# Five unused buffers that shift the operands of the expert stage's matmuls in a fused graph-attention and mixture-of-experts kernel

## The chip, the cores and the metric

One core of a Trainium2 chip runs the whole program. The metric is the device time of one execution in microseconds (us); less is better. The kernel before took 2409.39 us (median of 3 runs, 2408.38 to 2410.31).

## The reference

```python
def _L0_gnn_ref(h, adj, W, a):
    Wh = jnp.einsum('bnd,df->bnf', h, W)
    s1 = Wh @ a[:DOUT, 0]
    s2 = Wh @ a[DOUT:, 0]
    e = s1[:, :, None] + s2[:, None, :]
    e = jnp.where(e > 0, e, ALPHA * e)
    e = e + jnp.log(adj + EPS)
    alpha_w = jax.nn.softmax(e, axis=-1)
    return jnp.einsum('bij,bjf->bif', alpha_w, Wh)

def _L0_ffn_ref(x, Wr, br, W1, b1, g1, be1, m1, v1, W2, b2, g2, be2, m2, v2, Wo, bo):
    feat = jnp.mean(x, axis=0)
    w = jax.nn.softmax(feat @ Wr + br, axis=-1)
    h = jnp.einsum('bfd,edh->bfeh', x, W1) + b1
    h = jax.nn.relu(_bn(h, g1, be1, m1, v1))
    h = jnp.einsum('bfeh,ehk->bfek', h, W2) + b2
    h = jax.nn.relu(_bn(h, g2, be2, m2, v2))
    y = jnp.einsum('bfeh,ehd->bfed', h, Wo) + bo
    return jnp.einsum('bfed,fe->bfd', y, w)

x = x + _L0_gnn_ref(_layernorm(x), adj, W, a)
x = x + _L0_ffn_ref(_layernorm(x), ...)
```

x and adj are 128 graphs of 128 nodes, x with 256 features. There are 8 experts, and each has three layers of 256 by 256.

## The kernel before, in words

The kernel has two stages. The first stage is the graph attention. It goes over 32 groups of 4 graphs, with plain fp32 matmuls (the projection at L721, the product with the attention weights at L738, transposes at L692, L763 and L772), and it also splits the weights of layers 1 and 2 into a high and a low part of type float32r. The second stage is the expert stage. It goes over 32 tiles of 512 nodes and over 8 experts in each tile, so 256 units of work.

In the expert stage a product of two fp32 matrices is made of three float32r matmuls: high times high, high times low, low times high. They add up in PSUM. Per unit TensorE does:

- layer 1 in Strassen's form (`strassen`, L1189): 7 block products, each 3 matmuls of 256 columns, so 21. The stationary operand (loaded as weights) is a 128x128 block of `wq_hi` or `wq_lo`, the moving one is a 256-column block of `xq_hi` or `xq_lo`;
- layer 2 (`product`, L168): 12 matmuls of 512 columns. Stationary: a block of `w_hi` or `w_lo`; moving: `h1_hi` or `h1_lo`;
- layer 3 (`layer_3`, L1213): 24 matmuls of 256 columns. Stationary: a 128-column block of the activations `h2_hi` or `h2_lo`; moving: a 256-column block of `wo_hi` or `wo_lo`.

Once a tile, eight fp32 transposes (L129) prepare the next tile. Every matmul has a weight load of its own ahead of it (PEld in the profile), also where the same block follows twice. The three layers of different experts are interleaved by hand on TensorE: block 0 of layer 1 of the new expert, first half of layer 3 of the expert three before, blocks 1 to 4 of layer 1, second half of layer 3, block 5, layer 2 of the expert one before, block 6. Between them ScalarE and VectorE finish sums (`v`, L994; `z`, L1075 and L1085), apply batch norm and ReLU (`h`, L1002), split activations into high and low parts (L989 and L1092 for `h1`, L1008 and L1098 for `h2`) and add each expert's output (L1115). TensorE waits for each of these by a semaphore. `keep_clock` (L1199) issues matmuls whose result isn't used, at the start of the expert stage.

The matmuls of the three layers, as the code has them:

```python
mm = nc.tensor.matmul(out_ps, w[:, e, q, :], x[:, q, :], ...)            # L1189, layer 1
mm = nc.tensor.matmul(acc_ps, w[:, i, c, cols], s[:, c, :], ...)         # L168, layer 2
mm = nc.tensor.matmul(ps_y[:, b4, :], h[:, c, cols], w[:, e, c, :], ...) # L1213, layer 3
```

SBUF buffers are laid out one behind another in the order in which they are declared, each start rounded up to a multiple of 32 bytes within a partition. All blocks of one operand start at multiples of 512 bytes from the buffer's start, because a 128-column fp32 block is 512 bytes in a partition. So within a layer the distance between the start of the stationary block and the start of the moving block, modulo 512, is the same in every matmul.

Of the kernel before, what the change touches and what calls it, by code (L numbers as in the profile page):

```python
# [24 lines left out]
P = 128  # L25
# [13 lines left out]
def adj_ffn(nc, x, adj, gnn_w, gnn_a, wr, br, w1, b1, g1, be1, m1, v1, w2, b2, g2, be2, m2, v2, wo, bo, out):  # L39
# [17 lines left out]
    with ExitStack() as ctx:  # L57
        def sb(name, shape, dt=F32, stack=ctx):
            return stack.enter_context(nc.sbuf_tensor(name, shape, dt))
# [5 lines left out]
        ident = sb("ident", [P, P])  # L65
        minus_half = sb("minus_half", [P, 2 * EC])
        half_cols = sb("half_cols", [P, GB])
        wq_hi = sb("wq_hi", [P, E, Q, P], F32R)
        wq_lo = sb("wq_lo", [P, E, Q, P], F32R)
        w_hi = sb("w_hi", [P, E, C, D], F32R)  # L70
# [17 lines left out]
        acc = resb  # L88
        x1t = sb("x1t", [P, GB, D])
        xs = sb("xs", [P, Q + 1, H])  # L90
        xq_hi = sb("xq_hi", [P, Q, H], F32R)
        xq_lo = sb("xq_lo", [P, Q, H], F32R)

# [691 lines left out]
        with ExitStack() as sbk:  # L785
            def sbb(name, shape, dt=F32):
                return sb(name, shape, dt, sbk)
# [22 lines left out]
            bias_out = sbb("bias_out", [P, D])  # L810
            v = sbb("v", [P, 3, H])
            z = sbb("z", [P, C, T])
            h1_hi = sbb("h1_hi", [P, C, T], F32R)
            h1_lo = sbb("h1_lo", [P, C, T], F32R)
            ysum = x1[1]
            h2_hi = [sbb(f"h2_hi{i}", [P, C, T], F32R) for i in range(2)]
            h2_lo = [sbb(f"h2_lo{i}", [P, C, T], F32R) for i in range(2)]
            wo_hi = sbb("wo_hi", [P, E, C, D], F32R)
            wo_lo = sbb("wo_lo", [P, E, C, D], F32R)

# [488 lines left out]
```

## Time and profile before

| | before |
|---|---|
| median of 3 runs | 2409.39 us (2408.38 to 2410.31) |
| the profiled execution's own time | 2407.3 us |
| its span (first to last instruction) | 2405.5 us |
| mean granted TensorE clock | 0.997 of full speed |
| TensorE matmul busy | 2376.4 us, 99% |
| VectorE busy | 1688.0 us, 70% |
| ScalarE busy | 1611.6 us, 67% |
| GpSimd busy | 428.9 us, 18% |
| matmuls | 16217 |

The profile gives for each engine the time in which it worked, groups of instructions by line, and a chain of work that ended last. A matmul's record is longer than the time it takes up in a row of matmuls, since the next one starts before it ends: what counts for time is from one start to the next, or a piece of the chain divided by the number of matmuls in it.

### The profile page before, as it was taken

What the parts mean: (1) busy time and instruction counts of PE and PEld (TensorE: products, weight loads), DVE (VectorE), ACT (ScalarE), POOL (GpSimd) and SP (SyncE); (2) the same over time, 40 slices, a digit from 0 to 9 for tenths busy, and PEclk for the clock granted to TensorE, in tenths of its full rate; (3) what the DMA queues carried; (4) which work ended last, traced back from release to release, by engine and by line L of the source; (5) the groups of instructions that cost most, each with busy time, mean ns of one, the idle gap of its engine ahead of it and who ended that gap; (6) DMA issues with size and microseconds to landing.
All of it is one profiled execution on the core that took longest, in us unless ns stands there. A gap on an engine that the chain in (4) does not pass through costs nothing.

```text
span 2405.5 us, 46160 instructions
## 1 busy us (share of the span) xinstructions
PE 2376.4 (99%) x16217; PEld 2192.5 (91%) x16217; DVE 1688.0 (70%) x2582; ACT 1611.6 (67%) x2522; POOL 428.9 (18%) x562
## 2 busy tenths in 40 slices
PE   8999899999999999999999999999999999999999
PEld 7778799999999999999999999999999999999998
DVE  6999766666666676666666666666666666666666
ACT  6888566666666666666666666666666666666665
POOL 5888411111110000111111100101111111001010
PEclk9999899999999999999999999999999999999999
DMA  6778300000000000000000000000000000000000
GB/s 219 235 256 291 103 27 27 26 26 26 26 26 26 26 17 17 18 26 26 26 26 26 26 26 26 17 17 17 26 26 26 26 26 26 26 26 17 17 10 27
DMA packets 91330, 116.42 MB, mean 48 GB/s; under 512 B 4728, under 2 KB 78880, under 8 KB 91296
## 3 DMA queue, kind: packets, MB, share of 16 engines
q1 hardware_dynamic: 91296, 115.99, 14.9%
q8 instruction: 19, 0.31, 0.1%
q14 instruction: 15, 0.12, 0.0%
HBM read 82.42 MB, written 33.55 MB: 48 GB/s over the span
## 4 chain that ended last, share of the span: by engine, by line
PE 90%; DVE 5%; issue 2%; ACT 1%; POOL 1%; DVEq 0%; DMA 0%; SPq 0%; ACTq 0%; POOLq 0%
PE ps_y L1213 30%; PE ps_wide L168 30%; PE ps_wide L1189 26%; PE ps_wide L721 1%; PE ps_t L129 1%; DVE resb L613 1%; DVE st L573 1%; PE ps_th L738 1%; DVE h L647 1%; DVE st L565 1%; DVE w_bc L647 1%; DVE l_sb L626 1%; DVE p_sb L659 0%; POOL dev L417 0%; ACT xnT L553 0%
## 5 line engine op out<-in xcount | busy, mean ns | idle before, releaser
L994 ACT ACTIVATE v<-ps_wide,bn_cols 128x256 f32<-128x256 f32 x768 | 433.6, 565 | 398.7 <-PE ps_wide L1189 259.5
L1002 ACT ACTIVATE h<-ps_wide,bn_cols 128x512 f32<-128x512 f32 x512 | 399.0, 779 | 325.6 <-PE ps_wide L168 323.4
L1213 PE MATMUL ps_y<-wo_lo,h_hi 128*128 128x256 f32 x2048 | 578.1, 282 | 0.0
L1213 PE MATMUL ps_y<-wo_hi,h_hi 128*128 128x256 f32 x2048 | 576.7, 282 | 0.5 <-DVE h_lo L1098 0.5
L1213 PE MATMUL ps_y<-wo_hi,h_lo 128*128 128x256 f32 x2048 | 576.7, 282 | 0.0
L1092 DVE SCALAR_TENSOR_TENSOR h_lo<-z,h_hi 128x1024 fp32r<-128x1024 f32 x256 | 314.0, 1226 | 343.6 <-ACT h_hi L989 343.6
L1189 PE MATMUL ps_wide<-xq_hi,wq_hi 128*128 128x256 f32 x1792 | 509.8, 284 | 6.5 <-DVE z L1075 3.4
L1189 PE MATMUL ps_wide<-xq_hi,wq_lo 128*128 128x256 f32 x1792 | 506.0, 282 | 0.0
L1189 PE MATMUL ps_wide<-xq_lo,wq_hi 128*128 128x256 f32 x1792 | 505.8, 282 | 0.0
L168 PE MATMUL ps_wide<-h_hi,w_hi 128*128 128x512 f32 x1024 | 404.7, 395 | 0.6 <-DVE h_lo L1092 0.6
L168 PE MATMUL ps_wide<-h_hi,w_lo 128*128 128x512 f32 x1024 | 405.1, 396 | 0.0
L168 PE MATMUL ps_wide<-h_lo,w_hi 128*128 128x512 f32 x1024 | 403.7, 394 | 0.0
L1213 PEld LDWEIGHTS ps_y<-wo_hi,h_lo 128*128 128x128 f32 x2048 | 390.0, 190 | 0.0
L1213 PEld LDWEIGHTS ps_y<-wo_lo,h_hi 128*128 128x128 f32 x2048 | 389.0, 190 | 0.0
L1213 PEld LDWEIGHTS ps_y<-wo_hi,h_hi 128*128 128x128 f32 x2048 | 387.8, 189 | 1.1 <-DVE h_lo L1098 0.7
L1098 DVE TENSOR_TENSOR h_lo<-h,h_hi 128x1024 fp32r<-128x1024 f32 x256 | 313.4, 1224 | 99.0 <-ACT h_hi L1008 99.0
L973 POOL TENSOR_TENSOR resb<-resb,w_bc 128x512 f32<-128x512 f32 x64 | 86.7, 1356 | 1571.3 <-DMA resb<-x_scratch 1564.2
L1189 PEld LDWEIGHTS ps_wide<-xq_hi,wq_hi 128*128 128x128 f32 x1792 | 339.6, 190 | 18.6 <-DVE z L1075 3.9
L1189 PEld LDWEIGHTS ps_wide<-xq_hi,wq_lo 128*128 128x128 f32 x1792 | 338.6, 189 | 10.5
L1189 PEld LDWEIGHTS ps_wide<-xq_lo,wq_hi 128*128 128x128 f32 x1792 | 339.4, 189 | 0.0
L1115 DVE SCALAR_TENSOR_TENSOR resb<-ps_y,w_node,resb 128x512 f32<-128x512 f32 x448 | 332.9, 743 | 3.9 <-PE ps_y L1213 3.9
L1085 DVE SCALAR_TENSOR_TENSOR z<-ps_wide,bn_cols,v 128x512 f32<-128x512 f32 x256 | 191.9, 750 | 173.5 <-PE ps_wide L1189 173.4
(138 smaller groups left out, 2997.4 us busy)
## 6 DMA issues: line engine op xcount, KB each, us to landing
x_sb<-in_x SPq DMA_DIRECT2D x32, 512.0 KB, 4.1
res<-in_x SPq DMA_DIRECT2D x32, 512.0 KB, 6.0
x1t<-x_scratch SPq DMA_DIRECT2D x32, 512.0 KB, 3.3
resb<-x_scratch SPq DMA_DIRECT2D x32, 512.0 KB, 3.3
out<-resb SPq DMA_DIRECT2D x31, 512.0 KB, 3.0
adj_sb<-in_adj SPq DMA_DIRECT2D x32, 256.0 KB, 6.2
x_scratch<-h SPq DMA_DIRECT2D x16, 512.0 KB, 5.0
x_scratch<-w_bc SPq DMA_DIRECT2D x16, 512.0 KB, 4.8
```

Source lines behind the costliest of these rows:

```text
L129: last = nc.tensor.transpose(ps_x[:, c, b4 * N:(b4 + 1) * N], x1t[:, b4, c * P:(c + 1) * P], ident[:, :])
L168: mm = nc.tensor.matmul(acc_ps, w[:, i, c, cols], s[:, c, :], start=start and n == 0, stop=stop and n == len(terms) - 1)
L647: last = nc.vector.scalar_tensor_tensor(out=x1[q][:, b4, :], in0=ps_h[:, b4, :], scalar=rinv[:, b4:b4 + 1], in1=res[q][:, b4, :], op0=ALU. ...
L973: nc.gpsimd.tensor_tensor(resb[:, g, :], resb[:, g, :], ysum[:, g, :], ALU.add).then_inc(resb_done, 1)
L994: nc.scalar.activation(v[:, slot, :], ps_l1[:, 0, 0:H], ACT.Identity, bias=bn_cols[:, 1, cols], scale=bn_cols[:, 0, cols]).then_inc(done, 1)
L1002: nc.scalar.activation(h2[:, m, :], ps_l2[:, m, :], ACT.Relu, bias=bn_cols[:, 3, cols], scale=bn_cols[:, 2, cols]).then_inc(r2_done, 1)
L1085: nc.vector.scalar_tensor_tensor(out=z[:, 0, :], in0=ps_l1[:, 1, :], scalar=bn_cols[:, 0, C * e:C * e + 1], in1=v[:, 0:2, :].rearrange("p ...
L1092: nc.vector.scalar_tensor_tensor(out=h1_lo[:, :, :], in0=z[:, :, :], scalar=0.0, in1=h1_hi[:, :, :].bitcast(F32), op0=ALU.max, op1=ALU.sub ...
L1098: nc.vector.tensor_tensor(h2_lo[u[1] % 2][:, :, :], h2[:, :, :], h2_hi[u[1] % 2][:, :, :].bitcast(F32), ALU.subtract).then_inc(lo2_done, 1)
L1115: nc.vector.scalar_tensor_tensor(out=dst[:, g, :], in0=ps_y[:, g, :], scalar=w_node[:, e:e + 1], in1=old, op0=ALU.mult, op1=ALU.add).then_ ...
L1189: mm = nc.tensor.matmul(out_ps, w[:, e, q, :], x[:, q, :], start=start and n == 0, stop=stop and n == len(terms) - 1, skip_group_check=True)
L1213: mm = nc.tensor.matmul(ps_y[:, b4, :], h[:, c, cols], w[:, e, c, :], start=(k == 0 and b4 % per_bank == 0), stop=(k == len(terms) - 1 and ...
```

## The change

Five buffers are declared that nothing reads or writes. Each is put just ahead of an operand buffer and moves it and all that is declared behind it. No instruction is added, removed or put in another order; only addresses differ.

```diff
@@ -65,6 +65,7 @@
         half_cols = sb("half_cols", [P, GB])
+        sb("shift_wq", [P, 24])
         wq_hi = sb("wq_hi", [P, E, Q, P], F32R)
@@ -88,6 +89,7 @@
         xs = sb("xs", [P, Q + 1, H])
+        sb("shift_xq", [P, 80])
         xq_hi = sb("xq_hi", [P, Q, H], F32R)
@@ -810,11 +812,14 @@
             z = sbb("z", [P, C, T])
+            sbb("shift_h1", [P, 24])
             h1_hi = sbb("h1_hi", [P, C, T], F32R)
             h1_lo = sbb("h1_lo", [P, C, T], F32R)
             ysum = x1[1]
+            sbb("shift_h2", [P, 16])
             h2_hi = [sbb(f"h2_hi{i}", [P, C, T], F32R) for i in range(2)]
             h2_lo = [sbb(f"h2_lo{i}", [P, C, T], F32R) for i in range(2)]
+            sbb("shift_wo", [P, 112])
             wo_hi = sbb("wo_hi", [P, E, C, D], F32R)
```

Worked out from the declarations, the start of each operand within its partition, in bytes modulo 512 (the high and the low part are alike):

| layer | stationary, before | moving, before | stationary minus moving, before | stationary, now | moving, now | stationary minus moving, now |
|---|---|---|---|---|---|---|
| 1 | wq 288 | xq 416 | -128 | wq 384 | xq 320 | +64 |
| 2 | w 288 | h1 320 | -32 | w 384 | h1 320 | +64 |
| 3 | h2 320 | wo 320 | 0 | h2 384 | wo 320 | +64 |

Other buffers move too, by 96 bytes (`w_stage`, `x1t`, `resb`, `w_bc` and their neighbours) or by 416 (the first stage's `x_sb`, `res`, `adj_sb`, `wh`, `pT` and the rest of its own buffers). All starts stay multiples of 32 bytes.

## Rows read from the trace of the kernel before

**Rows 1.** The page's first part, and its slices for matmul and granted clock.

```profile
PE 2376.4 (99%) x16217; PEld 2192.5 (91%) x16217; DVE 1688.0 (70%) x2582; ACT 1611.6 (67%) x2522; POOL 428.9 (18%) x562
...
PEclk9999899999999999999999999999999999999999
```

**Rows 2.** Busy time by stretches: the first stage, and the expert stage.

```profile
core 0: us, PE busy (x) PEld busy (x) DVE busy (x) ACT busy (x) POOL busy (x), PEclk, DMA share, GB/s
...
0.00:262.00 262.00, 244.58 (x1313) 205.87 (x1314) 239.49 (x787) 206.79 (x558) 201.19 (x355) 0.99 0.76 241
300.00:2400.00 2100.00, 2099.14 (x14730) 1958.01 (x14729) 1420.46 (x1739) 1387.08 (x1935) 214.36 (x192) 1.00 0.07 24
```

**Rows 3.** The page's chain that ended last, by engine and by line.

```profile
PE 90%; DVE 5%; issue 2%; ACT 1%; POOL 1%; DVEq 0%; DMA 0%; SPq 0%; ACTq 0%; POOLq 0%
PE ps_y L1213 30%; PE ps_wide L168 30%; PE ps_wide L1189 26%; PE ps_wide L721 1%; PE ps_t L129 1%; DVE resb L613 1%; DVE st L573 1%; PE ps_th L738 1%; DVE h L647 1%; DVE st L565 1%; DVE w_bc L647 1%; DVE l_sb L626 1%; DVE p_sb L659 0%; POOL dev L417 0%; ACT xnT L553 0%
```

**Rows 4.** The page's groups of instructions: one of three alike for each layer.

```profile
L1213 PE MATMUL ps_y<-wo_lo,h_hi 128*128 128x256 f32 x2048 | 578.1, 282 | 0.0
...
L1189 PE MATMUL ps_wide<-xq_hi,wq_lo 128*128 128x256 f32 x1792 | 506.0, 282 | 0.0
...
L168 PE MATMUL ps_wide<-h_hi,w_lo 128*128 128x512 f32 x1024 | 405.1, 396 | 0.0
```

**Rows 5.** The chain in order of time (start, duration), pieces of one unit.

```profile
1002.61 1.44 PE ps_y L1213 x12
1004.05 1.42 PE ps_wide L1189 x12
1005.47 1.42 PE ps_y L1213 x12
1006.89 0.36 PE ps_wide L1189 x3
1007.25 2.80 PE ps_wide L168 x12
1010.05 0.71 PE ps_wide L1189 x6
```

**Rows 6.** The same chain where the transposes of the next tile stand.

```profile
1034.51 0.87 PE ps_t L129 x8
```

**Rows 7.** Instructions in order of time (start, duration), TensorE at half clock.

```profile
272.68 1.48 PE L1199 MATMUL ps_y<-xq_hi,wq_hi 128*128 128x256 f32 x6
273.96 0.41 PE L1189 MATMUL ps_wide<-xq_hi,wq_hi 128*128 128x256 f32 x1
```

**Rows 8.** Busy time of that stretch, with its granted clock.

```profile
272.50:275.50 3.00, 3.00 (x17) 3.00 (x17) 0.46 (x3) 1.13 (x2) 2.11 (x8) 0.56 0.60 190
```

**Rows 9.** Instructions in order of time, TensorE: first stage's projection, 16 fp32 matmuls.

```profile
102.53 3.65 PE L721 MATMUL ps_wide<-gw,xnT 128*128 128x258 f32 x16
106.02 0.75 PE L763 MATMUL ps_pT<-ident,p_sb 128*128 128x128 f32 x4
```

**Rows 10.** Instructions in order of time: last matmul of a layer 2, then transposes.

```profile
1034.12 0.39 PE L168 MATMUL ps_wide<-h_hi,w_lo 128*128 128x512 f32 x1
1034.34 1.04 PE L129 MATMUL ps_t<-ident,x1t 128*128 128x128 f32 x8
```

**Rows 11.** Weight loads of single lines: durations in ns, shortest/median/longest.

```profile
L1213 PEld LDWEIGHTS ps_y<-wo_hi,h_lo x1840: 187/192/193, 399.9 to 2300.0; 128*128 128x128 f32 x184
...
L168 PEld LDWEIGHTS ps_wide<-h_hi,w_hi x920: 187/188/188, 404.0 to 2298.2; 128*128 128x128 f32 x184
...
L129 PEld LDWEIGHTS ps_t<-ident,x1t x248: 137/141/146, 307.1 to 2290.8; 128*128 128x128 f32 x124
```

**Rows 12.** Instructions in order of time: TensorE and VectorE within one unit.

```profile
1005.31 0.27 PE L1213 MATMUL ps_y<-wo_hi,h_hi 128*128 128x256 f32 x1
1005.40 1.22 DVE L1092 SCALAR_TENSOR_TENSOR h_lo<-z,h_hi 128x1024 fp32r<-128x1024 f32 x1 [0.26 <-ACT h_hi L989]
1005.42 0.28 PE L1213 MATMUL ps_y<-wo_lo,h_hi 128*128 128x256 f32 x1
...
1007.09 0.39 PE L168 MATMUL ps_wide<-h_hi,w_hi 128*128 128x512 f32 x1
...
1008.34 0.74 DVE L1075 SCALAR_TENSOR_TENSOR z<-ps_wide,bn_cols,v 128x512 f32<-128x512 f32 x1
...
1009.89 0.28 PE L1189 MATMUL ps_wide<-xq_hi,wq_hi 128*128 128x256 f32 x1
```

## The prediction

> **What bounds the kernel now.** I read the page's first part, then the stretches, the chain, and last the chain's pieces in order of time. TensorE has a matmul in flight 99% of the span, at full granted clock nearly everywhere [rows 1]. The first stage, up to 262 us, leaves TensorE idle in places and has VectorE busy for 239 of 262 us; the expert stage has TensorE busy for 2099 of 2100 us, with VectorE at 1420 and ScalarE at 1387 [rows 2]. The chain is TensorE for 90%, and the three layers alone are 30 + 30 + 26% of it [rows 3]. So in the expert stage time is the number of matmuls times the spacing from one start to the next, and nothing else.
>
> The numbers: layer 3 has 3 x 2048 = 6144 matmuls, layer 1 has 3 x 1792 = 5376, both of 256 columns, and layer 2 has 3 x 1024 = 3072 of 512 [rows 4]. The spacing, from the pieces of one unit: layer 3 1.44 and 1.42 us for 12, so 118 to 120 ns; layer 1 1.42 for 12, 118 ns; layer 2 2.80 for 12, 233 ns [rows 5].
>
> What should these be? 256 columns at 2.4 GHz are 107 ns, 512 are 213. Three other rows run close to such a figure. Eight fp32 transposes, each with its weight load, take 0.87 us, 109 ns each [rows 6]; a plain fp32 matmul spends twice the time per column, so 128 columns there are 107 ns too. Sixteen fp32 matmuls of 258 columns take 106.02 - 102.53 = 3.49 us, 218 ns each, against 215 of columns [rows 9]. And layer 1's own kind of matmul, at the half clock (granted 0.56 in that stretch, so near the 1.2 GHz level), takes (273.96 - 272.68) / 6 = 213 ns, exactly its columns, with the operands 128 bytes apart as they always are [rows 7, 8]. **Only float32r at full clock loses time**: 9 to 11 ns in each matmul of 256 columns, and 233 - 216 = 17 ns in each of 512. Over the program that is 5376 x 9.4 + 6144 x 10.5 + 3072 x 17 = 51 + 65 + 52 = 168 us.
>
> What could lose it? During a matmul TensorE streams the moving operand, 4 bytes a column in each partition, and also loads the next stationary block: loads are in flight for 1958 of the 2100 us [rows 2]. At full clock float32r asks for 1024 bytes per 107 ns, twice what it asks in the rows without loss. The load fetches 512 bytes in at most the same time. If SBUF is divided into banks that repeat every 512 bytes, the moving stream, being twice as fast, runs through the load's bank about once per load, and where in the load this happens depends on the distance that the change sets. That is my mechanism; no row shows the banks themselves.
>
> **The change part by part.**
>
> *The five unused buffers.* No instruction is added or moved, on any queue, and no wait. Their direct cost is nothing.
>
> *Layers 1 and 3: the distance goes from -128 and from 0 to +64.* The trace has no matmul at +64 at full float32r rate, so I bound it. Below: 109 ns [rows 6]. Above: 0.12 us from start to start is common, and a load of layer 3 lasts up to 193 ns against 187 at its shortest [rows 11], so a load stretched in every matmul would give some 119 + 4 = 123 ns. Between them, the same code does reach 1005.42 - 1005.31 = 0.11 us [rows 12], so collisions aren't the same in each matmul and a better place exists. I take 115 ns, four below the mean of 119, between that good case and today's. That is 11520 x 4 = 46 us.
>
> *Layer 2: from -32 to +64.* Below: 216 ns, above 237 by the same stretch of 4 ns. One row stands nearest: the last matmul of layer 2 ahead of the transposes takes 1034.34 - 1034.12 = 0.22 us instead of 0.233 [rows 10], and what differs is that the load under it is a transpose's short one, 141 ns of record against 188 [rows 11]. So part of layer 2's loss hangs on the load, and about 4 ns of it is what a shorter overlap gives back; most of it doesn't go even then. I take 229 ns, 3072 x 4 = 12 us.
>
> *What is late next.* A faster TensorE shortens the cover of ScalarE's and VectorE's chains. Two are tight: `h1_lo` ends at 1005.40 + 1.22 = 1006.62 and layer 2 starts at 1007.09, 0.47 us later; `z` ends at 1009.08 and block 6 starts at 1009.89, 0.8 us later [rows 12]. The six pieces of a unit add up to 8.15 us [rows 5], and 4 ns in each of its 57 matmuls takes 0.23 us from the unit; less than half lies over either chain. So nothing is late. If the whole loss went (0.65 us per unit) the first would keep about 0.1 us. Cost nothing; if the cover were gone, 0.1 us in 256 units is 26 us.
>
> *First stage and other buffers.* Its fp32 matmuls run at 218 ns where 215 are columns [rows 9], and TensorE doesn't bound it. Buffers for DMAs move by 96 or 416 bytes; VectorE covers the DMAs there. I put it at 0, and 1 us to either side.
>
> **Sum.** 2407.3 (the profiled execution, 1.8 over its span) - 46 - 12 = 2349. That execution is 2 us below the median of the runs, so about 2351 beside the median; I say 2350.
>
> **The rivals.**
>
> *No effect.* The loss may belong to the stream and not to the load: a feed that can't quite keep 9.6 bytes per ns. For it: today's three distances, -128, -32 and 0, lose 9.4, 17 and 10.5 ns, and 17 on twice the columns is less than 2 x 10.5, so no distance stands out and the loss grows with columns [rows 5]. The long part of layer 2's loss that remains under a short load [rows 10] speaks the same way. Against: it has to explain why two matmuls of the same kind differ, 0.11 and 0.12 us. Time: 2407 to 2409. The Trainium skill, in "TensorE: Matmul & The Clock Gate", section "Step-by-step: what each phase is for", says that the moving operand and the weight load have independent SBUF read ports and that loading the next weights takes nothing from the running matmul. By that rule the change does nothing and the sum is 2407; the half-clock and fp32 rows agree with it, the full-clock float32r rows are its test.
>
> *The whole loss goes.* If +64 takes the two streams past each other altogether, each matmul falls to 109 or 216 ns: 2407 - 168 = 2239. For it: the rows without loss do reach these figures with loads under way. Against: a stream twice as fast as the load, over the length of a load, must meet it once in a period of 512 bytes wherever they start.
>
> *Slower: the moving stream starts right behind the load.* With the stationary block 64 bytes ahead in the bank order, the moving stream, which starts at about the same moment, may catch it in the first 64 bytes, in every matmul, and trail it. Price: 4 ns more in each, the spread of the load records [rows 11], 14592 x 4 = 58, so 2465, and half of that, 2436, if the collision costs only one of the two streams. The point from which it decides: whether the stream has already drawn 64 bytes (7 ns) when the load begins to read. For it: that distance lies nearest to a start in step. Against: layer 3 already has both starts equal, distance 0, and loses no more than layer 1 at -128.
>
> *The change doesn't do what it says.* The sizes (96, 320, 96, 64, 448 bytes) are multiples of 32, and the starts worked out from them give +64 in each layer. I give this nothing of its own.
>
> **How the numbers follow.** The forecast, some of the loss gone (2290 to 2395): 0.44. The whole or nearly the whole gone: 0.12. No effect: 0.22. Slower: 0.22. So faster by over 0.2% 0.56, within 0.2% (about 5 us, what a measurement of this kernel can tell from no change) 0.22, slower 0.22. Range: 2285 to 2440 takes in the forecast, no effect and the milder half of slower, and leaves out about 0.1 at either end. Signs on both sides hold much of the chance; the forecast's own range is 2290 to 2395.
>
> **What would show it.** Right: the piece of 12 layer 3 matmuls at 1.38 us, layer 1 the same, layer 2's at 2.75; TensorE still at 99% or so, with all the gain between 300 us and the end; load records at their shortest, 187 ns, everywhere. Wrong by no effect: the pieces read 1.42 and 2.80 again. Wrong by the slower rival: pieces of 1.47 and more, and loads of 193 ns or longer in all three layers. Wrong in the size: pieces near 1.31 and 2.60, and then waits on `h1_lo` ahead of layer 2. The first stage's end, near 262 us, should not move by more than 1 us.

## The result and the profile after

The changed kernel takes 2349.91 us (median of 4) against 2409.61 before: ratio 0.9755, 95% interval 0.9742 to 0.9768. One of its four executions took 2390.89 us and is left out of the ratio, as are one execution of the run with every start 32 bytes further (2394.13 us) and one of the last run (3873.8 us, at a granted clock of 0.556); none of the three has a trace. The profiled execution took 2350.85 us with a span of 2349.1, against 2407.3 and 2405.5.

Every line number after the first added buffer is one or more higher: layer 3 is now L1218, layer 1 L1194, layer 2 L170, the transposes L131.

The page's first part, and busy time by stretches (the lines that answer to [rows 1, 2]):

```profile
PE 2318.5 (99%) x16217; PEld 2134.5 (91%) x16217; DVE 1687.9 (72%) x2582; ACT 1608.8 (68%) x2522; POOL 426.8 (18%) x562
...
PEclk9999999999999999999999999999999999999999
```

```profile
0.00:262.00 262.00, 245.14 (x1309) 206.62 (x1310) 237.03 (x781) 205.48 (x553) 199.47 (x347) 0.99 0.76 241
262.00:300.00 38.00, 28.61 (x153) 23.82 (x152) 27.85 (x58) 17.43 (x32) 14.61 (x24) 0.91 0.26 83
300.00:2340.00 2040.00, 2039.63 (x14718) 1899.28 (x14717) 1418.93 (x1739) 1384.58 (x1937) 212.68 (x192) 1.00 0.07 24
```

TensorE still fills the expert stage (2039.63 of 2040 us), with the same work on VectorE and ScalarE (1419 and 1385 us against 1420 and 1387). No other engine has become the bound, and the gain is in the spacing of matmuls. But the records of neighbouring matmuls overlap, so a matmul that starts a little late leaves no gap in this busy time. The chain's pieces of one unit, against [rows 5]:

```profile
1000.04 1.36 PE ps_y L1218 x12
1001.40 1.36 PE ps_wide L1194 x12
1002.76 1.36 PE ps_y L1218 x12
1004.12 0.34 PE ps_wide L1194 x3
1004.46 2.79 PE ps_wide L170 x12
1007.25 0.69 PE ps_wide L1194 x6
```

Twelve matmuls of 256 columns take 1.36 us, 113.3 ns each, in layer 1 and in layer 3 alike; before it was 1.42 to 1.44. Layer 2 reads 2.79 against 2.80: it gained nothing. The unit is 7.90 us instead of 8.15, and 256 units of 0.25 us are 64 us, against 56.4 us of span.

The rest stands in three places. First, one unit of each tile, the fifth, starts its layer 2 late:

```profile
987.03 1.22 DVE L1097 SCALAR_TENSOR_TENSOR h_lo<-z,h_hi 128x1024 fp32r<-128x1024 f32 x1 [0.26 <-ACT h_hi L994]
...
988.38 0.19 PEld L170 LDWEIGHTS ps_wide<-h_hi,w_hi 128*128 128x128 f32 x1
988.39 0.49 PE L170 MATMUL ps_wide<-h_hi,w_hi 128*128 128x512 f32 x1
988.72 0.39 PE L170 MATMUL ps_wide<-h_lo,w_hi 128*128 128x512 f32 x1
```

`h1_lo` ends at 987.03 + 1.22 = 988.25 us, the first weight load of layer 2 starts at 988.38, and its second matmul starts 0.33 us after its first, where 0.23 is usual. This happens in all 31 tiles that follow transposes, each time with the first matmul 0.12 to 0.14 us behind the end of `h1_lo`, and costs 3.2 us in all. Before, only the very last layer 2 of the program started so.

Second, the transposes of the first tile (whose weight loads start at 307.1 us before) come later, because the first stage ended later in this execution:

```profile
L131 PEld LDWEIGHTS ps_t<-ident,x1t x248: 138/141/142, 308.4 to 2236.2; 128*128 128x128 f32 x124
```

That need not be an effect of the buffers. Two later runs (layer 2 at -64 and at 0 by moving h1) have every buffer of the first stage where it is here, and these loads start at 307.2 us in the one and at 308.9 us in the other.

Third, some units are slower again, although every address is what it was. The chain near the end:

```profile
2271.61 1.36 PE ps_y L1218 x12
...
2273.31 2.83 PE ps_wide L170 x12
...
2276.85 1.41 PE ps_y L1218 x12
```

From 2276.85 us on the same twelve matmuls of layer 3 take 1.41 us. That second figure, 1.41, turned out to be the key to the case. Counting shorter stretches of it near 374, 1634 and 1659 us, some 13 of the 256 units have it.

Summed over the start times in the two traces, from the first tile's transposes on, layer 1 takes 605.6 us where it took 633.0, layer 3 696.3 where it took 729.3, and layer 2 710.4 where it took 707.7. That is 57.7 us less, and with the start 1.4 us later it gives the 56.4 us (rounded) by which the spans differ.

### The profile page after: what moved, and what is told of

It is laid out like the page before. It is cut to its first block, busy times and chain, and to the rows that moved or that the text cites. A ratio compares the mean times of both kernels' runs of the same rounds, so it can differ in the third digit from the quotient of the medians.

```text
span 2349.1 us, 46160 instructions
## 1 busy us (share of the span) xinstructions
PE 2318.5 (99%) x16217; PEld 2134.5 (91%) x16217; DVE 1687.9 (72%) x2582; ACT 1608.8 (68%) x2522; POOL 426.8 (18%) x562
## 4 chain that ended last, share of the span: by engine, by line
PE 89%; DVE 5%; issue 2%; POOL 1%; DMA 1%; ACT 1%; DVEq 0%; SPq 0%; POOLq 0%; ACTq 0%
PE ps_wide L170 30%; PE ps_y L1218 30%; PE ps_wide L1194 26%; PE ps_wide L723 1%; PE ps_t L131 1%; DVE resb L615 1%; DVE st L575 1%; DVE st L567 1%; DVE h L649 1%; DVE w_bc L649 1%; PE ps_th L740 1%; DVE l_sb L628 1%; DVE p_sb L661 0%; DMA adj_sb<-in_adj 0%; POOL dev L419 0%
## 5 line engine op out<-in xcount | busy, mean ns | idle before, releaser
L1218 PE MATMUL ps_y<-wo_hi,h_hi 128*128 128x256 f32 x2048 | 566.0, 276 | 0.6 <-DVE h_lo L1103 0.6
L1218 PE MATMUL ps_y<-wo_lo,h_hi 128*128 128x256 f32 x2048 | 565.8, 276 | 0.0
L1218 PE MATMUL ps_y<-wo_hi,h_lo 128*128 128x256 f32 x2048 | 565.8, 276 | 0.0
L1097 DVE SCALAR_TENSOR_TENSOR h_lo<-z,h_hi 128x1024 fp32r<-128x1024 f32 x256 | 314.0, 1226 | 344.1 <-ACT h_hi L994 344.1
L1194 PE MATMUL ps_wide<-xq_hi,wq_hi 128*128 128x256 f32 x1792 | 501.0, 280 | 7.3 <-DVE z L1080 3.5
L1194 PE MATMUL ps_wide<-xq_hi,wq_lo 128*128 128x256 f32 x1792 | 496.0, 277 | 0.0
L1194 PE MATMUL ps_wide<-xq_lo,wq_hi 128*128 128x256 f32 x1792 | 495.9, 277 | 0.0
L170 PE MATMUL ps_wide<-h_hi,w_hi 128*128 128x512 f32 x1024 | 407.1, 398 | 0.8 <-DVE h_lo L1097 0.8
L170 PE MATMUL ps_wide<-h_hi,w_lo 128*128 128x512 f32 x1024 | 405.0, 396 | 0.0
L170 PE MATMUL ps_wide<-h_lo,w_hi 128*128 128x512 f32 x1024 | 404.9, 395 | 0.0
L1218 PEld LDWEIGHTS ps_y<-wo_hi,h_hi 128*128 128x128 f32 x2048 | 384.5, 188 | 1.2 <-DVE h_lo L1103 0.8
L1218 PEld LDWEIGHTS ps_y<-wo_lo,h_hi 128*128 128x128 f32 x2048 | 384.8, 188 | 0.0
L1218 PEld LDWEIGHTS ps_y<-wo_hi,h_lo 128*128 128x128 f32 x2048 | 384.5, 188 | 0.0
L1103 DVE TENSOR_TENSOR h_lo<-h,h_hi 128x1024 fp32r<-128x1024 f32 x256 | 313.3, 1224 | 66.9 <-ACT h_hi L1013 66.1
L1194 PEld LDWEIGHTS ps_wide<-xq_hi,wq_hi 128*128 128x128 f32 x1792 | 337.3, 188 | 19.2 <-DVE z L1080 4.2
L1194 PEld LDWEIGHTS ps_wide<-xq_hi,wq_lo 128*128 128x128 f32 x1792 | 337.7, 188 | 10.6
L1194 PEld LDWEIGHTS ps_wide<-xq_lo,wq_hi 128*128 128x128 f32 x1792 | 337.3, 188 | 0.0
```

The costliest lines, as they stand in the source:

```text
L1097: nc.vector.scalar_tensor_tensor(out=h1_lo[:, :, :], in0=z[:, :, :], scalar=0.0, in1=h1_hi[:, :, :].bitcast(F32), op0=ALU.max, op1=ALU.sub ...
L1103: nc.vector.tensor_tensor(h2_lo[u[1] % 2][:, :, :], h2[:, :, :], h2_hi[u[1] % 2][:, :, :].bitcast(F32), ALU.subtract).then_inc(lo2_done, 1)
L1194: mm = nc.tensor.matmul(out_ps, w[:, e, q, :], x[:, q, :], start=start and n == 0, stop=stop and n == len(terms) - 1, skip_group_check=True)
```

## The experiments

My theory at this point: each layer's spacing follows from its own distance, stationary start minus moving start modulo 512, and 256-column matmuls have a good place at +64. The first rivals: alignment of the starts, and a rhythm of the whole sequence that one layer sets for the others. All runs are the kernel before with buffers that nothing uses, unless said otherwise; the diffs show those buffers by name and size, and the buffer that follows each.

### Layer 3 alone

```diff
+            sbb("shift_h2", [P, 16])
             h2_hi = [sbb(f"h2_hi{i}", [P, C, T], F32R) for i in range(2)]
+            sbb("shift_wo", [P, 112])
             wo_hi = sbb("wo_hi", [P, E, C, D], F32R)
```

> Only layer 3 gets the distance +64 (h2 at 384, wo at 320 modulo 512); layer 1 stays at -128 and layer 2 at -32. Distance theory: the pieces of 12 layer 3 matmuls go from 1.42-1.44 to 1.36 us, layer 1 stays at 1.42 and layer 2 at 2.80; 6144 matmuls x 6.2 ns = 38 us, so about 2371 us. Rival, that one layer's addresses set the phase in which the whole sequence locks: layer 1 changes too. Rival, that the gain came from 64-byte alignment of the layer 1 weights (288 is no multiple of 64): nothing changes, 2409 us.

Measured: 2372.36 us, ratio 0.9853 (0.9836 to 0.9869). The pieces:

```profile
1000.17 1.37 PE ps_y L1215 x12
1001.54 1.41 PE ps_wide L1191 x12
...
1004.68 2.79 PE ps_wide L168 x12
```

Layer 3 gets most of what it has in the changed kernel, and the time is the one worked out for it alone. Layer 1 moved by about 0.01 us, which at this point looked like noise. It wasn't: summed over the trace, of 36.7 us less layer 3 has 26.6, layer 1 8.2 and layer 2 1.9, so the time came out for a partly different reason, and the rival that one layer's addresses change another layer's spacing had its first evidence here.

### All distances at +64, every start 32 bytes further

```diff
+        sb("shift_wq", [P, 32])
         wq_hi = sb("wq_hi", [P, E, Q, P], F32R)
+        sb("shift_xq", [P, 80])
         xq_hi = sb("xq_hi", [P, Q, H], F32R)
+            sbb("shift_h1", [P, 24])
             h1_hi = sbb("h1_hi", [P, C, T], F32R)
+            sbb("shift_h2", [P, 16])
             h2_hi = [sbb(f"h2_hi{i}", [P, C, T], F32R) for i in range(2)]
+            sbb("shift_wo", [P, 112])
             wo_hi = sbb("wo_hi", [P, E, C, D], F32R)
```

> All three distances are +64 as in the changed kernel, but every operand starts 32 bytes later, so that none is at a multiple of 64. Distance theory: as the changed kernel, pieces of 1.36, 1.36 and 2.79 us, 2350 us. Alignment theory: pieces back to 1.42 and more, 2405 us or above.

Measured: 2347.38, 2348.54 and 2351.37 us in three of four executions, ratio 0.9759 (0.9739 to 0.9779), pieces as in the changed kernel:

```profile
1001.14 1.36 PE ps_wide L1194 x12
1002.50 1.36 PE ps_y L1218 x12
...
1004.21 2.79 PE ps_wide L170 x12
```

No start is a multiple of 64 bytes here, and moving all operands on by 32 bytes together changes nothing. Alignment to 64 bytes is out: what counts is where operands lie to one another.

### All at -64, and a mixture

The sizes were chosen for the starts 352 (wq, w, h2) and 416 (xq, h1, wo).

```diff
+        sb("shift_wq", [P, 16])
         wq_hi = sb("wq_hi", [P, E, Q, P], F32R)
+        sb("shift_xq", [P, 112])
         xq_hi = sb("xq_hi", [P, Q, H], F32R)
+            sbb("shift_h1", [P, 24])
             h1_hi = sbb("h1_hi", [P, C, T], F32R)
+            sbb("shift_h2", [P, 112])
             h2_hi = [sbb(f"h2_hi{i}", [P, C, T], F32R) for i in range(2)]
+            sbb("shift_wo", [P, 16])
             wo_hi = sbb("wo_hi", [P, E, C, D], F32R)
```

> All three distances are -64, the mirror of the changed kernel. Theory that the sign matters (the stationary block has to lie ahead in the bank order): pieces of 1.42 us and more, 2405 us or above. Theory that only the distance from 0 matters: 1.36 us and 2350 us. For layer 2, which did not change between -32 and +64, I expect 2.80 again.

Measured: 2382.54 us (one execution), neither of the two times expected. Layers 1 and 3 at 1.41, layer 2 at 2.75:

```profile
1003.63 1.41 PE ps_y L1218 x12
1005.04 1.41 PE ps_wide L1194 x12
...
1008.22 2.75 PE ps_wide L170 x12
```

The mixture has wq and w at 384, xq at 352, h1 at 256, h2 at 416, wo at 320:

```diff
+        sb("shift_wq", [P, 24])
         wq_hi = sb("wq_hi", [P, E, Q, P], F32R)
+        sb("shift_xq", [P, 88])
         xq_hi = sb("xq_hi", [P, Q, H], F32R)
+            sbb("shift_h2", [P, 40])
             h2_hi = [sbb(f"h2_hi{i}", [P, C, T], F32R) for i in range(2)]
+            sbb("shift_wo", [P, 104])
             wo_hi = sbb("wo_hi", [P, E, C, D], F32R)
```

> Layer 1 at +32, layer 2 at +128, layer 3 at +96. If a collision costs the same wherever it falls, layer 1 and layer 3 read as at +64, 1.36 us for 12. If +64 is a narrow good place, one of the two or both go back to 1.42 us. Layer 2: 2.80 us if its loss belongs to the moving stream, less if it depends on the distance and +128 is a good place. Each piece is read by itself; the time is then 2350 to 2410 us.

Measured: 2398.59 us (one execution): layer 1 at +32 reads 1.41 to 1.42, layer 3 at +96 1.41 to 1.44, layer 2 at +128 2.80. So +64 looked like a narrow good place for 256 columns, and -64 like a better one for layer 2, 4 ns a matmul. I had expected layer 2 to stay at 2.80 there: a miss.

### Each layer at its best distance

```diff
+        sb("shift_wq", [P, 24])
         wq_hi = sb("wq_hi", [P, E, Q, P], F32R)
         wq_lo = sb("wq_lo", [P, E, Q, P], F32R)
+        sb("shift_w", [P, 96])
         w_hi = sb("w_hi", [P, E, C, D], F32R)
+        sb("shift_xq", [P, 112])
         xq_hi = sb("xq_hi", [P, Q, H], F32R)
```

(h1, h2 and wo get the buffers of the changed kernel.)

> Layers 1 and 3 at +64 as in the changed kernel, layer 2 at -64, where the run with all distances at -64 had its shortest spacing (229 ns against 233 to 234 at -32 and +64). Distance theory, each layer by itself: pieces of 1.36 us for layers 1 and 3, 2.75 for layer 2, so 3072 x 4.7 = 14 us less than the changed kernel: 2335 us. Rival, that layer 2's spacing hangs on the phase in which layer 1 hands over: 2.79 again, 2350 us.

Measured: 2384.73 us, ratio 0.9893 (0.9876 to 0.9909): 35 us slower than the changed kernel, where 14 us less was expected.

```profile
1001.92 2.76 PE ps_wide L171 x12
...
1005.38 1.41 PE ps_y L1219 x12
1006.80 1.41 PE ps_wide L1195 x12
```

Layer 2 has what was hoped for. But layers 1 and 3, at the same +64 as in the changed kernel, are back at 1.41. **Here the theory that each layer follows its own distance fell.**

### The old distances, exchanged, and three new ones

```diff
+        sb("shift_xq", [P, 96])
         xq_hi = sb("xq_hi", [P, Q, H], F32R)
+            sbb("shift_h1", [P, 24])
             h1_hi = sbb("h1_hi", [P, C, T], F32R)
+            sbb("shift_h2", [P, 104])
             h2_hi = [sbb(f"h2_hi{i}", [P, C, T], F32R) for i in range(2)]
+            sbb("shift_wo", [P, 32])
             wo_hi = sbb("wo_hi", [P, E, C, D], F32R)
```

> The distances of before change places: layer 1 at 0, layer 2 at 0, layer 3 at -128. Distance theory: layer 1 then reads what layer 3 had at 0 (120 ns where it runs long), layer 3 what layer 1 had at -128 (118 to 120). Theory that the layers differ by what they do: each keeps its own figure. Time about 2405 us in both; layer 2 at 0 is new, between 229 and 236 ns.

Measured: 2384.15 us (one execution), where 2405 was expected. Layers 1 and 3 read 1.42 and 1.43, as before, and layer 2 at 0 reads 2.73, the shortest so far. Most of the gain is layer 2's: (2.80 - 2.73) / 12 is 5.8 ns, times 3072 is 18 of the 25 us.

```profile
1003.01 1.43 PE ps_y L1217 x12
1004.44 1.42 PE ps_wide L1193 x12
...
1007.63 2.73 PE ps_wide L169 x12
```

The next has xq at 480, h1 at 96, h2 at 64, and the rest as before:

```diff
+        sb("shift_xq", [P, 16])
         xq_hi = sb("xq_hi", [P, Q, H], F32R)
+            sbb("shift_h1", [P, 56])
             h1_hi = sbb("h1_hi", [P, C, T], F32R)
+            sbb("shift_h2", [P, 120])
             h2_hi = [sbb(f"h2_hi{i}", [P, C, T], F32R) for i in range(2)]
+            sbb("shift_wo", [P, 64])
             wo_hi = sbb("wo_hi", [P, E, C, D], F32R)
```

> Layer 1 at -192, layer 2 at +192, layer 3 at -256 (the same as +256). If the banks repeat every 256 bytes, layer 1 at -192 is the same as +64 and reads 1.36 us for 12, and layer 3 at -256 the same as 0, 1.43 us. If they repeat every 512 and +64 is a single good place, both read 1.40 to 1.44. Layer 2 at +192 equals -64 under a period of 256 and would read 2.75 us; otherwise 2.78 to 2.83.

Measured: 2377.08 us (one execution). Layer 1 at -192 1.37, layer 3 at -256 1.42 to 1.43, layer 2 at +192 2.76. All three are what a period of 256 bytes would give. But after the run before this one a single figure no longer stands for a distance, so I don't take the period as shown; it stays open. Layer 1 reads 1.37 here between pieces of layer 3 at 1.42 and more, as layer 3 alone at +64 read 1.37 between pieces of layer 1 at 1.41: a layer can take up its short spacing anew within the unit.

### A short load under each third matmul

Addresses as before. Layers 1 and 3 are changed in the same way. The output rows 32 to 127 miss the second of each three terms.

```diff
-                mm = nc.tensor.matmul(acc_ps, w[:, i, c, cols], s[:, c, :], ...)
+                wide = P if n % 3 != 1 else 32
+                mm = nc.tensor.matmul(acc_ps[0:wide], w[:, i, c, m * P:m * P + wide], s[:, c, :], ...)
```

> Addresses as in the kernel before. The second of each three matmuls in all three layers loads and computes only 32 of its 128 stationary columns, so that 96 of 128 output rows miss the product of the terms that it carries; all matmuls stream as many columns as before. Under the first of each three the load is then a short one. Theory that the loss is a collision of the moving stream with the load: the spacing after the first of three falls to about 109 ns (256 columns) and 216 ns (512), the others stay near 119 and 233. Rival, a feed too slow for float32r at full clock whatever is loaded: 119 and 233 ns everywhere.

Measured: 2386.27 us (one execution), pieces of 1.41, 1.41 and 2.78. Matmuls of layer 2 in order of time:

```profile
1000.34 0.39 PE L169 MATMUL ps_wide<-h_hi,w_hi 128*128 128x512 f32 x1
1000.57 0.40 PE L169 MATMUL ps_wide<-h_lo,w_hi 128*32 128x512 f32 x1
1000.80 0.40 PE L169 MATMUL ps_wide<-h_hi,w_lo 128*128 128x512 f32 x1
1001.04 0.40 PE L169 MATMUL ps_wide<-h_hi,w_hi 128*128 128x512 f32 x1
```

The short load (a record of 108 ns against 188) runs under the first matmul, which takes 0.23 us to the next start, like its neighbours. The average over the trace from 400 to 2200 us is finer: 229.8 ns, against 233.3 and 232.8 for the other two. So in layer 2 a load of 32 columns instead of 128 gives back some 3 ns of the 17, where a collision with the load should have given back all. In layers 1 and 3 the first of three takes 117.2 and 118.3 ns, where that theory wanted 109. Neither theory's numbers hold. Shortening loads did take 23 us off the whole, so loads aren't without effect either; whether by their length or by the rhythm that the next section finds, this run doesn't show.

### Only layer 2's weights back to +64

```diff
+        sb("shift_wq", [P, 24])
         wq_hi = sb("wq_hi", [P, E, Q, P], F32R)
+        sb("shift_stage", [P, 96])
         w_stage = sb("w_stage", [P, Q + 1, P])
+        sb("shift_xq", [P, 112])
         xq_hi = sb("xq_hi", [P, Q, H], F32R)
```

(as the run with each layer at its best, with the 384 bytes behind `w_lo` instead of ahead of `w_hi`)

> As the run best_per_layer, which kept layers 1 and 3 at +64 and yet lost their gain (2384.7 us), except that layer 2's weights go back to +64; every other operand, the transposes' input too, lies at exactly the addresses of that run. If layer 2's distance is what spoils the other layers: pieces of 1.36 us again and 2350 us. If it was something else (the distance modulo 1024, the place of the transposes' input): 2385 us and pieces of 1.41 again.

Measured: 2370.35 us (one execution), halfway between the two times that were expected, and the chain says why. Pieces of one execution, end of one tile, transposes, start of the next:

```profile
1015.56 1.41 PE ps_wide L1195 x12
1016.98 1.41 PE ps_y L1219 x12
1018.39 0.35 PE ps_wide L1195 x3
1018.74 2.79 PE ps_wide L171 x12
1021.54 0.87 PE ps_t L132 x8
1022.41 0.70 PE ps_wide L1195 x6
1023.11 1.36 PE ps_y L1219 x12
1024.47 1.36 PE ps_wide L1195 x12
...
1081.25 1.36 PE ps_y L1219 x12
1082.95 2.79 PE ps_wide L171 x12
1085.74 0.87 PE ps_t L132 x8
1087.32 1.41 PE ps_y L1219 x12
1088.73 1.41 PE ps_wide L1195 x12
```

From 1023.11 to 1081.25 us all 24 pieces of twelve 256-column matmuls read 1.36, across seven layers 2. At the very same addresses the next tile runs at 1.41, and so on in turn, with the change at the transposes each time from 437 us on. So at +64 matmuls of 256 columns have **two rhythms**, 113.3 and 117.5 ns, and mostly keep the one they are in. Layer 2 at +64 mostly hands on either rhythm unchanged; the transposes, with another kind of load and stream, often change it.

It isn't a law, as the changed kernel's own trace shows: 29 of its 31 transposes are followed by the short rhythm. Twice it falls into the long one in the middle of a tile, and both times right behind a layer 2 that started late for `h1_lo` (its pieces read 2.90 us at 1630.55 and 2.83 at 2273.31), but most of the late ones leave the short rhythm as it is. And twice it goes back to the short one across an ordinary layer 2 (at 379 and 1664 us).

### Layer 2 at -64 and at 0 by moving h1

The changed kernel's other buffers stay; the one ahead of `h2_hi` gets the size that keeps h2 at 384.

```diff
+            sbb("shift_h1", [P, 56])
             h1_hi = sbb("h1_hi", [P, C, T], F32R)
+            sbb("shift_h2", [P, 112])
             h2_hi = [sbb(f"h2_hi{i}", [P, C, T], F32R) for i in range(2)]
```

> The changed kernel with layer 2 at -64 reached by moving its moving operand h1 (448) instead of its weights. Layers 1 and 3 keep +64 and layer 1's buffers keep their addresses. Theory that TensorE locks into one of two rhythms at +64 and that layer 2 hands over the wrong one: 1.41 us pieces and 2385 us as in best_per_layer. Theory that each layer follows its own distance: 1.36 and 2.75 us, 2336 us.

Measured: 2378.56 us (one execution), near the 2385 of the two-rhythm theory. In its trace the first unit of each of the 31 tiles is in the short rhythm and the other seven in the long one, and 31 units of 45 matmuls x 4.2 ns are the 6 us between the two figures. In the second variant the buffer ahead of `h1_hi` is `[P, 40]`, and there is none ahead of `h2_hi`:

> The changed kernel with layer 2 at 0, where another run gave its shortest spacing (226 to 227 ns), by moving h1 to 384. If layers 1 and 3 stay in the rhythm of 113.3 ns: 3072 x 6.5 = 20 us less than the changed kernel, 2330 us. If the hand-over from layer 2 puts them in the other rhythm of 117.8 ns: 11520 x 4.5 = 52 us more, less those 20, about 2382 us.

Measured: 2373.57 us, ratio 0.9849 (0.9833 to 0.9866). The unit after the transposes, and the next:

```profile
1025.59 1.36 PE ps_y L1217 x12
1026.94 1.36 PE ps_wide L1193 x12
...
1030.01 2.73 PE ps_wide L170 x12
...
1033.45 1.41 PE ps_y L1217 x12
1034.86 1.41 PE ps_wide L1193 x12
1036.27 1.41 PE ps_y L1217 x12
```

The transposes put this tile, and every second one, in the short rhythm, and the first layer 2 at distance 0 ends it: layer 2 itself runs at 226.7 ns (2.72 to 2.73 us), and hands over the long one. The transposes' input lies where the changed kernel has it, so its place isn't what makes tiles alternate.

### Layer 2 at 0 by its weights

```diff
+        sb("shift_w", [P, 112])
         w_hi = sb("w_hi", [P, E, C, D], F32R)
+        sb("shift_stage", [P, 16])
         w_stage = sb("w_stage", [P, Q + 1, P])
```

(beside the buffers of the changed kernel)

> Layer 2 at 0 again, but by moving its weights (320) and not h1; the transposes' input lies as in the changed kernel modulo 512. In the step from layer 2 back to layer 1 the stream of h1 (320) now meets a load of wq (384), +64, where it was 0 in the run l2_zero. If the rhythm of 113.3 ns is lost because of that step's distance, it now holds over all tiles and the time is 2330 us. If it is lost because of the distance inside layer 2, each tile has it for one unit at most and the time is about 2373 us again.

Measured: 2374.72, 2382.46 and 2383.52 us in three of four executions, ratio 0.9890 (0.9868 to 0.9911). The trace is of the first, with pieces of 1.41 and 2.75; the first unit of each of its 31 tiles is in the short rhythm and the rest in the long one. So the distance in the step back to layer 1 isn't what ends the short rhythm. In all four runs where layer 2 had another distance than +64 beside two layers at +64, it ran faster inside and the short rhythm was gone after one layer 2 at the latest; whether its speed or its distance does that isn't separated. And layer 2 at 0 reads 2.75 here and 2.73 in the run before, so its own distance alone doesn't fix its spacing either. No version tried beats the changed kernel. That one gives up some 20 us in layer 2 and keeps the 48 of the short rhythm (11520 x 4.2 ns).

## Why the prediction was right

**What bounds it** held: TensorE has a matmul in flight nearly throughout, and all the gain lies between 300 us and the end.

**The time was right to 1 us, and that was luck.** The terms of the sum erred against each other: 46 + 12 = 58 us were forecast and 56.4 came, but as 60.4 in layers 1 and 3, 2.6 lost again in layer 2, and 1.4 of later start.

- *Layers 1 and 3, 4 ns each, 46 us.* Over the trace 27.4 and 33.0 us, so 5.1 and 5.4 ns each. The bound from below (109 ns) isn't reached: 113.3 stays.
- *Layer 2, 4 ns each, 12 us.* Wrong. Its pieces read 2.79 against 2.80, where the sign asked for was 2.75, and over the trace it takes 2.6 us more: 0.6 less by its spacing, 3.2 more by the late starts. The term came from a last matmul of layer 2 that takes 0.22 us (229 ns by its unrounded start times) above a transpose's short load [rows 10], read as "4 ns is what a shorter overlap gives back". The change makes no load shorter; and in the changed kernel the same matmul above the same short load takes 1014.99 - 1014.75 = 0.24 us.

```profile
1014.75 0.40 PE L170 MATMUL ps_wide<-h_hi,w_lo 128*128 128x512 f32 x1
1014.99 1.04 PE L131 MATMUL ps_t<-ident,x1t 128*128 128x128 f32 x8
```

- *First stage, 0 with 1 us to either side.* It ended 1.4 us later, within what executions with the same addresses there differ by (307.2 and 308.9 us).
- *Nothing late next, cost nothing.* Wrong, by 3.2 us. The step that failed is "less than half lies over either chain". The time from the end of `h1_lo` to the first matmul of layer 2 is 1.18 us in most units before and 0.94 us now: the whole 0.25 us of a unit came off it. In the tightest unit, the one that the prediction had read at 0.47 us [rows 12], it fell to 0.13 us with layer 2 starting 0.1 us late. The price was there, as "if the cover were gone, 0.1 us in 256 units"; it fell due in one unit of eight. The busy share of 2039.63 in 2040 us hides it.

**The mechanism** was right in its first half: the relative place of operands changes the spacing, with no instruction changed, and a move of all by 32 bytes doesn't. Its second half, one collision per load at a place that the distance fixes, was wrong: the same addresses give 113.3 or 117.5 ns according to what ran before. The 0.11 us from which the prediction took that "a better place exists" is no sign of either: in that trace a spacing of 112 or 113 ns in layer 3 stands only behind the first matmul of a half that follows layer 1, once in every unit, so it belongs to the hand-over. Banks and collisions themselves were not seen; that a short load under a matmul of layer 2 gives back 3 ns of 17 speaks against their simplest form. Nor is it separated whether the other engines' accesses take part, since the buffers also move for them; VectorE's records are as long as before (`h1_lo` 1226 ns and `h2_lo` 1224 on average, in both).

**The rivals.** No effect fell. The Trainium skill says in "TensorE: Matmul & The Clock Gate", section "Step-by-step: what each phase is for", that loading the next weights takes nothing from the running matmul. By that rule, as the prediction read it, addresses alone don't move the time, and here they moved it by 2.4%. Whether it is the load that takes from the matmul, or which part of the path is shared, the runs don't show. The whole loss gone: no, 4 ns above 109 stay in 256 columns and 17 above 216 in 512. Slower by a collision at the start: not at +64; the load records of layer 3, 187 to 193 ns before [rows 11], now read 188 in the median:

```profile
L1218 PEld LDWEIGHTS ps_y<-wo_hi,h_lo x2048: 187/188/192, 300.6 to 2345.4; 128*128 128x128 f32 x187
```

## What to carry to other kernels

Where TensorE is without a gap and float32r matmuls at full clock take more than their columns (here 118 to 120 ns for 256, 107 being columns), the spacing can be tuned by unused buffers alone: 0.25 us of an 8.15 us unit here. Read twelve matmuls of each kind from the chain's pieces and not the busy time, and test a new layout in the whole sequence: a layer's best distance by itself (layer 2 at 0 or at -64) cost 24 to 35 us in all, because it put its neighbours in a worse rhythm. Read a wait from start to start too, in the tightest unit of a tile: matmul records overlap, and the busy share showed nothing of 3.2 us. And look at several executions: a rhythm that is kept and not forced may be the other one next time.

## What the runs showed of the hardware that was not expected

- *Two rhythms at the same addresses.* 256-column float32r matmuls with their loads run at 113.3 or at 117.5 ns in the same execution (1.36 and 1.41 us for 12), keep it over dozens of matmuls and mostly through a layer 2 at +64, and change mostly at the transposes. The changed kernel's own last units are in the long one. The 2390.89 us of one of its executions, and the 2394.13 us of one with every start 32 bytes further, would fit a stay there from start to end (2350 + 11520 x 4.2 ns less what is in it already and less the late starts is some 2393 us, an estimate); without a trace of either that is only argued. They are two of the eight executions that have all three layers at +64.
- *Steps.* The steady spacings are 113.3 and 120 ns (1.44 us for 12, before) for 256 columns and 226.7 ns (2.72) for 512: the columns' time plus one, two and two times 6.7 ns, that is 16 cycles of 2.4 GHz. The long rhythm of 117.5 lies between, as do layer 2's 229 to 234 ns in other runs, so the steps may be a coincidence of three figures.
- *Layer 2 follows its distance more closely, though not exactly:* 2.75 at -64, 2.80 at -32, 2.72 to 2.75 at 0, 2.79 at +64, 2.80 at +128, 2.76 at +192.
